# Graph stage: relu of the messages on ScalarE, low parts of the embedding on GpSimd

## What is computed

```python
x = x + _L0_gnn_ref(_layernorm(x), adj, ...)      # degree-normed aggregate, relu
x = x + _L0_ffn_ref(_layernorm(x), ...)           # one linear layer
x = x + _L1_gnn_ref(_layernorm(x), adj, ...)      # below
x = x + _L1_ffn_ref(_layernorm(x), ...)           # 30 iterations of tanh, silu, layernorm, linear

def _L1_gnn_ref(x, mask, ...):
    h = relu(bn(conv1d(x, conv1_w, 0)))
    x_conv = relu(bn(conv1d(h, conv2_w, 8)) + x)          # 17 taps
    s = x @ w_se.T + b_se                                 # 3 numbers per node
    dist = sq[:, :, None] + sq[:, None, :] - 2 * s @ s.T
    A = exp(-dist) * mask
    msg = relu(x @ w_msg.T + b_msg)
    x_nmp = A @ msg
    # GRU cell on (x_conv, x_nmp) and x: gates r, z, n
    return (1 - z) * n + z * x
```

## Time and profile before

| | |
|---|---|
| median of 3 runs | 1390.7 us (1389.99 to 1391.48) |
| the profiled execution's own time | 1390.53 us |
| its span | 1388.6 us |
| TensorE busy | 1332.4 us (96%) |
| VectorE busy | 1234.2 us (89%) |
| ScalarE busy | 1011.1 us (73%) |
| GpSimd busy | 948.3 us (68%) |

### The profile page before, as it was taken

The page is one execution under the profiler, slowest core; times in us unless marked ns, Lnnn a source line. Parts: engine busy times, 40 slices in busy tenths (PEclk is TensorE's granted clock), DMA queues, the critical chain, the costliest instruction groups (busy, mean ns, idle before and its releaser), DMA issues.

```text
span 1388.6 us, 28231 instructions
## 1 busy us (share of the span) xinstructions
PE 1332.4 (96%) x8786; PEld 1085.0 (78%) x8786; DVE 1234.2 (89%) x2774; ACT 1011.1 (73%) x1373; POOL 948.3 (68%) x749
## 2 busy tenths in 40 slices
PE   4899999999999999869999999999999999999998
PEld 3677777777777776558888888888888888888887
DVE  6678888887788886599999999999999999999997
ACT  1344444444444444569999999999999999999994
POOL 2244444444444444269999999999999999999995
PEclk9899999999999999969999999999999999999999
DMA  5111111111111100000000000000000000000004
GB/s 178 39 39 38 38 38 38 38 38 38 38 38 38 37 0 1 0 1 0 0 0 0 0 0 0 0 0 0 0 0 0 0 0 0 0 0 0 0 0 122
DMA packets 29790, 27.68 MB, mean 20 GB/s; under 512 B 3269, under 2 KB 21448, under 8 KB 29640
## 3 DMA queue, kind: packets, MB, share of 16 engines
q1 hardware_dynamic: 29768, 27.41, 6.2%
HBM read 23.21 MB, written 4.19 MB: 20 GB/s over the span
## 4 chain that ended last, share of the span: by engine, by line
PE 78%; DVE 11%; issue 4%; ACT 3%; POOL 1%; SPq 1%; DMA 0%; DVEq 0%; ACTq 0%; POOLq 0%
PE psum L751 34%; PE psum L763 15%; PE psum L747 6%; PE psum L553 4%; PE psum L555 4%; PE psum L554 4%; PE psum L694 3%; PE psum L570 2%; PE psum L575 2%; ACT emb_f L855 2%; PE psum L584 2%; DVE emb_n L1177 1%; DVE x_less_n L1161 1%; PE psum L564 1%; DVE xh L1059 1%
## 5 line engine op out<-in xcount | busy, mean ns | idle before, releaser
L751 PE MATMUL psum<-w_t,y_all 128*128 128x128 f32 x3840 | 493.7, 282 | 0.0
L751 PEld LDWEIGHTS psum<-w_t,y_all 128*128 128x128 f32 x3840 | 447.9, 192 | 54.5 <-issue 54.5
L454 POOL TENSOR_TENSOR f_rs<-f_var,half_neg 128x8 f32<-128x8 f32 x240 | 410.4, 1710 | 49.2 <-DVE f_var L1116 30.2
L1091 DVE BATCH_NORM_STATS2 f_stat<-g_ring 128x6 f32<-128x256 f32 x960 | 340.7, 413 | 3.9 <-ACT g_ring L813 3.9
L458 POOL TENSOR_TENSOR h_ring<-g_ring,f_rs 128x640 f32<-128x640 f32 x240 | 302.5, 1260 | 18.8
L1107 DVE SCALAR_TENSOR_TENSOR u_ring<-t_ring,psum 128x1024 f32<-128x1024 f32 x232 | 278.1, 1199 | 0.0
L763 PE MATMUL psum<-ident,h_ring 128*128 128x128 f32 x1920 | 250.6, 274 | 6.4 <-DVE h_ring L1080 6.4
L813 ACT ACTIVATE g_ring<-u_ring 128x1024 f32<-128x1024 f32 x240 | 253.5, 1056 | 0.8 <-DVE u_ring L1107 0.8
L836 ACT ACTIVATE y_all<-psum 128x1024 f32<-128x1024 f32 x240 | 243.7, 1015 | 8.4 <-PE psum L763 8.4
L822 ACT ACTIVATE t_ring<-psum 128x1024 f32<-128x1024 f32 x232 | 238.6, 1029 | 13.5 <-PE psum L751 4.9
L763 PEld LDWEIGHTS psum<-ident,h_ring 128*128 128x128 f32 x1920 | 219.1, 142 | 7.1 <-issue 3.8
(11 more groups left out here) (158 smaller groups left out, 1774.3 us busy)
## 6 DMA issues: line engine op xcount, KB each, us to landing
work<-in_adj_dram SPq DMA_DIRECT2D x16, 1024.0 KB, 5.4
x_tok<-in_x_dram SPq DMA_DIRECT2D x16, 256.0 KB, 5.5
out_dram<-y_all SPq DMA_DIRECT2D x8, 512.0 KB, 3.3
work<-in_L_gnn_conv_w_dram SPq DMA_DIRECT2D x1, 1088.0 KB
work<-in_L_gnn_w_ih_dram SPq DMA_DIRECT2D x1, 384.0 KB
work<-in_L_gnn_w_hh_dram SPq DMA_DIRECT2D x1, 192.0 KB
work<-in_L_gnn_W_dram SPq DMA_DIRECT2D x1, 64.0 KB, 5.1
work<-in_L_ffn_weight_dram SPq DMA_DIRECT2D x1, 64.0 KB, 4.8
```

What stands on the lines that cost most here:

```text
L454: pool.tensor_tensor(f_rs[:, j % 4, :], f_var[:, j % 2, :], half_neg[:, 0:GT], ALU.pow).then_inc(f_pow, 1)
L751: m = pe.matmul(y_ps[k % 2][:, h, C * t:C * t + C], y_all[:, GT * k + NT * h + t, :], w1_t[:], start=False, stop=True, skip_group_check=True)
L1091: ins = dve.bn_stats(f_stat[:, j % 2, q, :], both)
```

## The change

The relu of the messages moves from GpSimd to ScalarE, behind the two copies that make the embedding's high parts. The three subtractions that make the low parts move from VectorE to GpSimd, to the place where the relu was. Each of them now raises `s_emb_lo` by itself and GpSimd waits for each before it goes on, so the waits for that semaphore count three per graph. A `settle` (a count of a semaphore nobody waits for) goes with the relu.

```diff
@@ gpsimd, step @@
-                    pool.wait_ge(s_msg_pre, b + 1)
-                    wait(pool, s_nmp, b)
-                    settle(pool, s_passed_pool)
-                    pool.tensor_scalar(msg_tok[:], msg_pre[:], 0.0, None, ALU.max).then_inc(s_msg_tok, 1)
+                    pool.wait_ge(s_emb_hi, 2 * b + 2)
+                    for i, (m, emb, first, last) in enumerate(((0, emb_m, 2, 4), (1, emb_n, 1, 2), (1, emb_n, 3, 4))):
+                        rows = slice(QUAD * first, min(QUAD * last, KD))
+                        pool.tensor_tensor(emb[rows, :], emb_f[m][0][rows, :], emb[rows, :].bitcast(F32),
+                                           ALU.subtract).then_inc(s_emb_lo, 1)
+                        pool.wait_ge(s_emb_lo, 3 * b + i + 1)
@@ tensor, dist @@
-                        pe.wait_ge(s_emb_lo, b + 1)
+                        pe.wait_ge(s_emb_lo, 3 * b + 3)
@@ scalar, step @@
-                    wait(act, s_emb_lo, b)
+                    wait(act, s_emb_lo, 3 * b)
...
                         act.activation(emb[:], emb_f[m][0][:], ACT.Copy).then_inc(s_emb_hi, 1)
+                    act.wait_ge(s_msg_pre, b + 1)
+                    wait(act, s_nmp, b)
+                    act.activation(msg_tok[:], msg_pre[:], ACT.Relu).then_inc(s_msg_tok, 1)
                     exp(b, 0)
@@ vector, step @@
-                if l1:
-
-                    dve.wait_ge(s_emb_hi, 2 * b + 2)
-                    for m, emb, first, last in ((0, emb_m, 2, 4), (1, emb_n, 1, 2), (1, emb_n, 3, 4)):
-                        rows = slice(QUAD * first, min(QUAD * last, KD))
-                        ins = dve.tensor_tensor(emb[rows, :], emb_f[m][0][rows, :], emb[rows, :].bitcast(F32), ALU.subtract)
-                    ins.then_inc(s_emb_lo, 1)
```

## The result

| | before | with the change |
|---|---|---|
| median | 1391.09 us (4 runs) | 1402.68 us (1402.02 to 1403.64, 4 runs) |
| ratio | | 1.0085, 95% interval 1.0067 to 1.0102 |
| profiled execution: own time, span | 1390.53, 1388.6 us | 1402.17, 1400.2 us |

The kernel became slower by 11.6 us, by the medians and by the spans alike. Forecast were 1403.8 us and +13.2.

What follows compares the result with a forecast made beforehand. TensorE's work plus its stalls was taken to bound the graph stage. Full steps +10.8, first step +1.3 and last step +1.1 made +13.2 us, so 1403.8 us, range 1390 to 1409.

Steps and rivals of the forecast that it cites:

- That TensorE alone counts in the graph stage, and loses at two places: Graph stage time is TensorE's work plus stalls; near the change it stalls at `turn(1)`, 0.68 us, and `dist(0)`, 0.16 us.
- What could be won: Both TensorE stalls of a full step, at `turn(1)` and `dist(0)`: at most 0.84 us, 11.8 us in 14 steps.
- The exclusion: VectorE and GpSimd instructions with two SBUF inputs each shut each other out; whichever started first goes first, delaying `dist(0)` 1.45 us.
- 1.28 us a subtraction, whatever the rows: Each low-part subtraction on GpSimd takes 1.28 us without interference; fewer rows make it no cheaper.
- Relu on ScalarE for nothing: The messages' relu fits ScalarE's 4.24 us idle time before `dist(0)` and costs nothing; without that cover 0.6 to 0.7 per step.
- per full step +0.77: Each of 14 full steps: `dist(0)` 1.45 us late, less the 0.68 us stall removed at `turn(1)`; +10.8 us in all.
- The first `dist(0)`: In the first step, `dist(0)` starts at 62.43 us instead of 61.16, behind GpSimd's three subtractions: +1.3 us.
- In the last step: TensorE, already waiting 1.46 us for the low parts, waits longer; the third subtraction follows without an exchange: +1.1 us.
- its delay alone costs nothing: The update's last VectorE instruction, shut out, ends at 297.22 instead of 296.55; TensorE needs its result only at 298.12.
- No exclusion: Rival: GpSimd subtractions and VectorE instructions run freely side by side; sum -2.3 us, 1388.4 us; chance 0.11.
- half of it: Rival: only one exchange between VectorE and GpSimd per full step instead of two; 1398 us; chance 0.13.
- The clock did not fall: Judges the rival that a 1.6 us stall lowers the clock in every full step: 24 us more, 1428 us; chance 0.04.

Runs made afterwards that it cites:

- relu_alone: The kernel before the change, with only the relu moved to ScalarE and the subtractions left on VectorE: 1386.24 us, ratio 0.9966 to before.
- one_sbuf_input: The changed kernel, with two VectorE instructions beside the subtractions reading PSUM, so one SBUF input each: 1394.13 us, ratio 1.0025 to before.
- two_subs_vector: The kernel before, with the relu on ScalarE and two subtractions instead of three, still on VectorE: 1375.19 us, ratio 0.9893 to before.
- subs_alone: The changed kernel, with the relu back on GpSimd behind the subtractions: 1406.30 us, ratio 1.0108 to before.

## Why the prediction was right

*That TensorE alone counts in the graph stage, and loses at two places.* Right. The changed kernel's step is longer by 0.66 us, and A, B and C explain it: +1.44, -0.71 and -0.09 make +0.64.

*What could be won.* A little too small. The prediction let the four transposes ahead of `dist(0)` take 0.44 us; with nothing to wait for they take 0.36 (A in relu_alone), and B is then 5.45. So the kernel before lost 0.25 at `dist(0)` and not 0.16, and 0.70 at `turn(1)`: 0.95 per step and not 0.84. The sum goes by differences of starts and isn't touched by this.

*The exclusion.* Right, and shown by one_sbuf_input. Forecast for the update's last instruction 1.65 us, measured 1.66; aggregate's second 0.93, measured 1.06; from the transposes to `dist(0)` 2.05, measured 2.05. The rule was read from two overlaps in the earlier trace rows, and over the fourteen full steps the 42 subtractions all lie between 1.58 and 1.71 us. With two of three exchanges taken away, 8.6 of the 11.6 us came back; what is left is 3.1 us against before. Of that the full steps have only 0.05 us each, since there the stall at `turn(1)` that the change buys off is nearly as large as what GpSimd's slower arithmetic and the first exchange cost; the rest lies outside them.

*1.28 us a subtraction, whatever the rows.* Right: 1.27 for 9 rows, 1.29 for 32, and 1.28 for 41 in the one step where nothing interferes.

*Relu on ScalarE for nothing.* Right, and it is more than that: relu_alone shows a gain of 4.7 us. The prediction had its mechanism (0.69 instead of 0.98) but counted it inside the sum.

*The size.* +13.2 forecast, +11.6 measured. The step that was mis-sized is "per full step +0.77": it was 0.66. What is missing is C, 0.09 us in 14 steps, some 1.3 us: the prediction followed VectorE to `turn(1)` and not to the next place at which TensorE waits for it. The first `dist(0)` came at 62.41 us (forecast 62.43), +1.25. In the last step TensorE's waits up to `dist(0)` grew by 1.0 us (forecast +1.1), but not as the sum had it: 0.66 of it is wait for the update, whose last instruction was shut out there too, and 0.35 wait for the low parts. The prediction had said of that instruction that its delay alone costs nothing, which is so in the full steps only. VectorE, at the end of step 14, before and after (timeline):

```profile
567.12 0.69 DVE L1168 SCALAR_TENSOR_TENSOR upd<-x_less_n,n_act 128x512 f32<-128x512 f32 x1
577.21 1.64 DVE L1173 SCALAR_TENSOR_TENSOR upd<-x_less_n,n_act 128x512 f32<-128x512 f32 x1
```

That these parts add up to 11.5 is in part luck. Followed through the two traces, the 11.6 us of the spans are +1.40 up to step 1, +8.55 over thirteen steps, +0.43 in step 14 without its wait for the update (its wait for `x_conv_l` fell from 1.23 to 0.97), +1.0 in the last step up to `dist(0)`, -0.3 behind it, and +0.5 in the iteration stage, which the change leaves as it was. There the clock stayed at 1.2 GHz for longer: over 5 us from the first products on the granted clock was 0.50 (623 to 628 us), before 0.68 (612 to 617). Why it was so no run shows.

*The rivals.* No exclusion and half of it are excluded by the trace. The clock did not fall: from 50 to 560 us the granted clock is 1.00 with a stall of 1.6 us in each step.

```profile
50.00:560.00 510.00, 488.23 (x2277) 366.98 (x2278) 366.68 (x661) 226.05 (x377) 255.57 (x261) 1.00 0.09 31
```

## What to carry to other kernels

Idle time of an engine is not room for work: GpSimd had 5 us free in each step, but what it was given could not read beside VectorE's two-input instructions, and both grew. Before such a move look for one overlap of each kind in the trace and read off who ended when. Prefer the move that takes an instruction that reads SBUF off GpSimd while VectorE has two-input ones to run (here the relu to ScalarE, which even with its single input had slowed one down: 4.7 us at no cost that the trace shows), or feed VectorE from PSUM where they run side by side. And a stall in front of an engine is worth what the chain behind the next stall allows: savings at two waits that one chain feeds don't add.

## What the hardware showed unexpectedly

A GpSimd subtraction of 9 rows takes as long as one of 32, 1.27 and 1.29 us for 512 columns, so there instructions count and not rows; on VectorE it is 0.68 us each in two_subs_vector, for 9 and for 32 rows.

Making VectorE wait for the subtractions before one of its instructions was faster than letting it run beside them (1400.5 against 1402.7 us).

In the last graph step TensorE fell to 1.2 GHz after its stalls, for 8 matmuls of the convolution's taps in the kernel before, 6 in the changed kernel, 11 in subs_alone and 12 in one_sbuf_input, though the changed kernel and subs_alone have the same stall of 1.8 us ahead; in two_subs_vector it didn't fall between `dist(0)` and `dist(2)`. Each such matmul costs 0.2 us. What decides their number is open, and it blurs comparisons of these kernels by about 1 us. The start blurs them more: with the same work up to there, the first copy into `emb_n` began at 57.32 us in the kernel before and at 60.44 in relu_alone, which had the half clock for longer.
